# A graph network with two feed-forwards on one core: the last phase with its row preparation placed among the feed-forward's chunks, and the choice of rows by a search for the threshold

## What is computed

```
# _L1_gnn_ref, the end (out: 3125 x 4 heads x 64, divided by the sum of the edge weights)
out = jax.nn.elu(out + b)
x = x + out.reshape(N, 256)

# _L1_ffn_ref on the layer-normed x (b = 1, s = 3125)
weights = x @ wr + br
k = max(1, int(0.5 * s));  kk = k - 1                 # 1561 rows are kept
idx = top_k(weights, k)[:kk]                          # ties: the earlier row first
h = gelu(x[idx] @ w1 + b1);  y = (h @ w2 + b2) * weights[idx]
out = x_normed + (y put at idx, 0 elsewhere)          # and the layer's input is added to it
```

## Time and profile before

| | |
|---|---|
| median of 3 runs | 2442.72 us (2441.84 to 2443.51) |
| the profiled execution | 2447.71 us, its span 2446.0 us |
| busy in the span | PE 1842.6, DVE 1503.4, POOL 1372.5, ACT 627.9 us |
| last phase | from about 2152 us to the end |

### The profile page before, as it was taken

One profiled execution on the slowest core, in us unless ns is written; L12 is line 12 of the kernel. 1 busy time (PEld: TensorE's weight loads), 2 busy tenths in 40 slices (PEclk: granted clock), 3 DMA queues, 4 the chain that ended last, 5 costly groups with the idle time before them and its releaser, 6 DMA issues. The chain is left out here.

```text
span 2446.0 us, 37019 instructions
## 1 busy us (share of the span) xinstructions
PE 1842.6 (75%) x9564; PEld 1312.8 (54%) x9565; DVE 1503.4 (61%) x3325; ACT 627.9 (26%) x1252; POOL 1372.5 (56%) x1387
## 2 busy tenths in 40 slices
PE   2879999988997977109999995368888888811687
PEld 2667777763443447106666663256566566601366
DVE  7666644447557867713333333647777777678698
ACT  4000000004546654513333332121111111111342
POOL 3777777762777740464445445847777777632000
PEclk8565555558998987559999998569988989855798
DMA  7333333333002024321111111321111111300100
GB/s 226 105 101 103 105 104 104 105 97 116 1 1 54 1 75 158 97 75 35 37 35 39 37 37 44 89 64 28 28 28 28 28 28 28 27 5 0 26 26 28
DMA packets 113005, 144.03 MB, mean 59 GB/s; under 512 B 46718, under 2 KB 82430, under 8 KB 112822
## 3 DMA queue, kind: packets, MB, share of 16 engines
q0 software_dynamic: 60160, 86.81, 14.8%
q1 hardware_dynamic: 52787, 56.58, 7.7%
HBM read 114.00 MB, written 29.18 MB: 59 GB/s over the span
## 5 line engine op out<-in xcount | busy, mean ns | idle before, releaser
L497 PE MATMUL psA<-oh,G 128*128 128x128 f32 x1568 | 444.9, 448 | 64.0 <-DMA G<-xn_d,gat_i 34.3
L595 POOL DMA_INDIRECT rec_d<-rec,posd x392 | 393.4, 1004 | 167.2 <-issue 124.6
L1500 POOL DMA_INDIRECT g<-tab_d,recs x416 | 395.8, 951 | 148.6 <-issue 126.5
L312 POOL DMA_INDIRECT G<-xn_d,gat_i x392 | 379.5, 968 | 146.4 <-issue 138.8
L497 PEld LDWEIGHTS psA<-oh,G 128*128 128x128 f32 x1568 | 351.2, 312 | 157.5 <-issue 98.3
L1649 PE MATMUL psS<-vv,oh 128*125 128x260 f32 x832 | 290.1, 496 | 92.7 <-DVE acc L1581 92.5
L840 PE MATMUL psZ<-z,W 128*128 (+1 forms) x1344 | 264.1, 359 | 26.0 <-DVE z L739 26.0
L447 DVE TENSOR_TENSOR accT<-accT,psA 128x256 f32 x392 | 165.0, 421 | 170.4 <-PE psA L497 144.3
L1649 PEld LDWEIGHTS psS<-vv,oh 128*125 128x125 f32 x832 | 162.1, 226 | 190.7 <-DVE acc L1581 163.0
L642 ACT ACTIVATE z<-psZ,vec 128x500 f32 (+2 forms) x112 | 70.8, 634 | 643.1 <-PE psZ L833 533.3
L1246 PE MATMUL psH<-we,xh 128*128 x1344 | 215.1, 310 | 0.7 <-issue 0.6
(11 more groups left out here) (257 smaller groups left out, 2760.1 us busy)
## 6 DMA issues: line engine op xcount, KB each, us to landing
raw<-in_L_ffn_w SPq DMA_DIRECT2D x16, 682.0 KB, 10.2
xs_d<-zero SPq DMA_DIRECT2D x1, 7168.0 KB, 23.8
xs<-xs_d SPq DMA_DIRECT2D x56, 128.0 KB, 2.1
y_d<-yv POOLq DMA_DIRECT2D x56, 128.0 KB, 2.0
g<-tab_d,recs POOLq DMA_INDIRECT x416, 2.5
G<-xn_d,gat_i POOLq DMA_INDIRECT x392, 2.7
rec_d<-rec,posd POOLq DMA_INDIRECT x392
raw<-in_L_ffn_w SPq DMA_DIRECT2D x16, 384.0 KB, 10.1
```

The lines of the kernel that those rows point to most:

```text
L312: pool.indirect_dma_start(out=G[:, i, :], out_offset=None, in_=xn_d, in_offset=bass.IndirectOffsetOnAxis(ap=gat_i[:, t:t + 1], axis=0)).th ...
L497: last = nc.tensor.matmul(psA[i // 2][:, i % 2, h, :], G[:, i, 128 * h:128 * (h + 1)], oh[:, i, :], start=True, stop=True)
L595: pool.indirect_dma_start(out=rec_d.rearrange("p (t r) -> (p t) r", r=2), out_offset=bass.IndirectOffsetOnAxis(ap=posd[:, t:t + 1], axis=0 ...
L1500: pool.indirect_dma_start(out=g3[:, n % BODY, j, :], out_offset=None, in_=tab_d, in_offset=bass.IndirectOffsetOnAxis(ap=recs[:, t, 1:2], a ...
```

## The change

Phase 6 is written anew; the numbers of its operations per block stay as they are, but the order and some engines change.

- The five small loads are issued by SP at the start of phase 5.
- VectorE divides and adds `bgb` + 1 (it now does the add as well) for all five groups first (`lift`), ACT takes exp(og - 1) (`lifted`, four buffers `eg`). Then `fold(c)` finishes the ELU in two operations and makes mean and variance of group c; `spread`, `scales6` and `norm` give the square root (ACT), reciprocal, its value plus 1 and the offset (VectorE), and the normed rows (ACT, no longer VectorE). `twice(c)`, on ACT, makes x2 + xn4 as x2 (1 + 1/sd) - mean/sd in place of POOL's add.
- Only group 0 is prepared ahead of the feed-forward. Group c + 1 is prepared during chunk c (c < 4), its parts placed behind fixed m in each queue. Blocks are turned in pairs.
- The ranks and the trip through memory are gone. From chunk 4 on a search finds the value of the KEPT-th logit: one round counts the logits of one sign, eight rounds find the bits of the value, 3 and then 4 at a time; in each VectorE counts over its 25 logits a row for 7 or 15 candidates, and TensorE sums over the rows by a matmul with ones (`total`). A last round counts the values above and settles ties. Count, total and the reading of it are placed one m apart.
- `finish` is split: `lower` frees `psD` at once, and `finish` of blocks 0 to 15 follows in chunk 5, of 16 to 24 at the end.
- The downs of chunk 0 stand in front of chunk 1's ups; from chunk 2 on they stand among the ups as before. The writes of the output go in two parts, partitions 0 to 111 and 112 to 124.

The core of the diff (tile addresses, semaphores and the single operations of the search are left out):

```diff
@@ phase 5
+            @block.sync
+            def _(sp):
+                sp.dma_start(bgb[:, :], a["L1_gnn_b"].partition_broadcast(PB)).then_inc(s_b6, 16)
...
@@ phase 6, sync
-                sp.wait_ge(s_wv, 1)
-                    sp.dma_start(w_d.rearrange("o (b p) -> p (o b)", p=PB), wv[:, :]).then_inc(s_wd, 16)
-                sp.wait_ge(s_wd, 16)
-                sp.dma_start(wb[:, :], w_d[0, :].partition_broadcast(PB)).then_inc(s_wbl, 16)
                 for b0, n in CHUNKS:
                     sp.wait_ge(s_fin, b0 + n)
-                    sp.dma_start(ov[:, b0:b0 + n, :], outb[:, b0:b0 + n, :]).then_inc(s_out, 16)
+                    for lo, hi in SPLIT:
+                        sp.dma_start(ov[lo:hi, b0:b0 + n, :], outb[lo:hi, b0:b0 + n, :]).then_inc(s_out, 16)
@@ gpsimd: both loops of adds are gone; it fills less1, earlier, ones6 and tab
@@ scalar
+                def lifted(c):
+                    act.wait_ge(s_og, c + 1)
+                    if c >= 4:
+                        act.wait_ge(s_fold, c - 3)
+                    nc.scalar.activation(eg[:, c % 4, :, :], og[:, 5 * c:5 * c + 5, :], ACT.Exp, bias=less1[:, :]).then_inc(s_eg, 1)
+                def spread(c):
+                    act.wait_ge(s_v6, c + 1)
+                    nc.scalar.activation(sd6[:, 5 * c:5 * c + 5], mv6[:, 5 * c:5 * c + 5, 1], ACT.Sqrt).then_inc(s_d6, 1)
+                def norm(c):
+                    act.wait_ge(s_sc6, c + 1)
+                    for b in range(5 * c, 5 * c + 5):
+                        nc.scalar.activation(xn4[:, b, :], x2[:, b, :], ACT.Identity, bias=nm6[:, b:b + 1],
+                                             scale=rs6[:, b:b + 1]).then_inc(s_n6, 1)
+                for c in range(5):
+                    lifted(c)
+                spread(0)
+                norm(0)
+                for g in range(3):
+                    high_x(g)
                 for c, (b0, nb) in enumerate(CHUNKS):
                     for m in range(FM):
...
+                        if c < 4:
+                            if m == 1:
+                                spread(c + 1)
+                            if m == 2:
+                                norm(c + 1)
+                            if m == 4:
+                                high_x(3 * c + 3)
+                                high_x(3 * c + 4)
+                            if m == 6:
+                                high_x(3 * c + 5)
+                        if c < 5 and m == 7:
+                            twice(c)
@@ vector
+                def lift(c):
+                    ch.step(nc.vector.tensor_tensor(o_, v[:, hs, 0:OD], den[:, hs].unsqueeze(2).to_broadcast([PB, 5 * NH, OD]),
+                                                    ALU.mult))
+                    nc.vector.tensor_tensor(o_, o_, bgb[:, :].unsqueeze(1).to_broadcast([PB, 5 * NH, OD]), ALU.add).then_inc(s_og, 1)
+                def fold(c):
+                    ch.step(nc.vector.scalar_tensor_tensor(e_, e_, 1.0, og[:, cs, :], ALU.min, ALU.max))
+                    ch.step(nc.vector.scalar_tensor_tensor(x2[:, cs, :], e_, -1.0, x2[:, cs, :], ALU.add, ALU.add))
+                    dve.sem_inc(s_fold, 1)
+                    for b in range(5):
+                        ch.mark(nc.vector.bn_stats(bst6[:, b, :], x2[:, 5 * c + b, :]))
...
+                def digit_count(k):
+                    ch.step(nc.vector.tensor_tensor(met[:, 0:n, :], mag[:, :].unsqueeze(1).to_broadcast([PB, n, NB]),
+                                                    now.unsqueeze(2).to_broadcast([PB, n, NB]), ALU.is_ge))
+                    nc.vector.tensor_reduce(cn[:, 0:n], met[:, 0:n, :], AX_X, ALU.add).then_inc(s_cn, 1)
+                def digit_known(k):
+                    dve.wait_ge(s_cs, k + 2)
+                    ch.step(nc.vector.tensor_scalar(met[:, 0, 0:n], psC[:, 0:n], few[:, 2:3], 0.0, ALU.is_ge, ALU.add,
+                                                    accum_out=few[:, 3:4]))
...
                     for m in range(FM):
+                        fine(c, m, n)
                         n += 1
+                        if c < 4:
+                            if m == 0:
+                                fold(c + 1)
+                            if m == 1:
+                                scales6(c + 1)
+                            if m == 3:
+                                logits(c + 1)
+                            if m == 4:
+                                low_x(3 * c + 3)
+                                low_x(3 * c + 4)
+                            if m == 6:
+                                low_x(3 * c + 5)
+                        if c >= 2 and m % 2 == 1:
+                            lower(b0 - CB + m // 2)
+                        k = (c - SEARCH) * FM + m
+                        if k == 0:
+                            sign_count()
+                        if k == 1:
+                            sign_known()
+                            digit_count(0)
+                        if 2 <= k <= len(DIGITS):
+                            digit_known(k - 2)
+                            digit_count(k - 1)
+                        if k == ROUNDS:
+                            digit_known(ROUNDS - 2)
+                            last_count()
+                        if k == ROUNDS + 1:
+                            chosen()
+                        if k > ROUNDS + 1 and k - ROUNDS - 2 < b0 // CB - 1:
+                            for b in range(CB * (k - ROUNDS - 2), CB * (k - ROUNDS - 1)):
+                                finish(b)
@@ tensor
+                def total(r):
+                    n = 1 if r == 0 else DIGITS[r - 1][1] if r < ROUNDS else 1 + NB
+                    pe.wait_ge(s_cn, r + 1)
+                    last = nc.tensor.matmul(psC[:, 0:n], ones6[:, :], cn[:, 0:n], start=True, stop=True)
...
                 for c, (b0, nb) in enumerate(CHUNKS):
+                    if c == 1:
+                        for b in range(CB):
+                            down(b)
                     for m in range(FM):
+                        up(c, m, n)
                         n += 1
-                        if c and m % 2 == 1:
+                        if c >= 2 and m % 2 == 1:
                             down(b0 - CB + m // 2)
+                        if c < 4 and m == 3:
+                            turn6(3 * c + 3)
+                            turn6(3 * c + 4)
+                        if c < 4 and m == 5:
+                            turn6(3 * c + 5)
+                        r = (c - SEARCH) * FM + m - 1
+                        if 0 <= r <= ROUNDS:
+                            total(r)
```

More of the change, by code:

```diff
@@ new lines, in program @@
+        ones6 = at("ones6", o, [PB, PB]); o += 512
+        DIGITS = [(28, 7)] + [(sh, 15) for sh in range(24, -1, -4)]
+        tab = at("tab", o, [PB, len(DIGITS), 16], I32); o += 512
+        cand = at("cand", o, [PB, 16], I32); o += 64
+        met = at("met", o, [PB, 16, NB]); o += 1600
+        cn = at("cn", o, [PB, 1 + NB]); o += 128
+        few = at("few", o, [PB, 8]); o += 32
+        dig_i = at("dig_i", o, [PB, 1], I32); o += 32
+        pre_i = at("pre_i", o, [PB, 1], I32); o += 32
@@ L1755, in _ @@
+                nc.gpsimd.memset(less1[:, :], -1.0).then_inc(s_k6, 1)
+                ch.n += 1
                 ch.step(nc.gpsimd.memset(earlier[:, :], 1.0))
[L1756 to L1767, removed]
+                ch.step(nc.gpsimd.affine_select(out=earlier[:, :], in_=earlier[:, :], compare_op=ALU.is_gt, fill=0.0,
+                                                base=0, pattern=[[1, PB]], channel_multiplier=-1))
+                ch.step(nc.gpsimd.memset(ones6[:, :], 1.0))
@@ L1769, in _ @@
+                for k, (sh, n) in enumerate(DIGITS):
+                    ch.step(nc.gpsimd.tensor_scalar(tab[:, k, 0:n], iota[0:PB, 1:1 + n], float(1 << sh), None, ALU.mult))
             @block.scalar
             def _(act):
-                for c in range(5):
[L1772 to L1781, removed]
@@ new lines, in norm, with twice @@
+                def norm(c):
[3 more added lines that the diff above has]
+                                             scale=rs6[:, b:b + 1]).then_inc(s_n6, 1)
+                def twice(c):
+                    for b in range(5 * c, 5 * c + 5):
+                        nc.scalar.activation(x2[:, b, :], x2[:, b, :], ACT.Identity, bias=nm6[:, b:b + 1],
+                                             scale=rp6[:, b:b + 1]).then_inc(s_x6, 1)
@@ L1783, in _, with high_x @@
+                def high_x(g):
+                    act.wait_ge(s_t6, g + 1)
+                    t, cols = turned(g)
+                    nc.scalar.activation(xt6[:, 0, :, cols], t, ACT.Copy, scale=XS).then_inc(s_th, 1)
+                act.wait_ge(s_k6, 1)
+                for c in range(5):
+                    lifted(c)
[3 more added lines that the diff above has]
+                    high_x(g)
                 n = 0
-                act.wait_ge(s_b6, 80)
@@ new lines, in finish @@
```

(18 more changed lines are left out.)

253 lines of the change are left out of this document (150 added, 103 removed).

## The result

The changed kernel takes 2362.3 us (median of 4 runs, 2360.0 to 2364.0), 0.9667 of the kernel before (95% interval 0.965 to 0.9684). The forecast was 2366. A second measurement gave 0.9658 (0.9645 to 0.9671). The profiled execution took 2362.4, its span 2360.7.

A forecast was written before the change was run, and what follows sets the result against it. VectorE was taken to set the feed-forward's pace, after 115 us before the first gelu. Steps from 2152.4 plus 3 for the clock reached 2369.5, 76.5 under 2446.0; off the 2442.7 median, 2366 us; 8-in-10 range 2350 to 2396.

The forecast's parts named there:

- head, to the first up: Start of the last phase: no wait for loads, only group 0 prepared; 27.4 us, first up-projection at 2179.8.
- chunk 0: First feed-forward chunk: three engines take turns, 21.8 us, then four downs alone; 38.3 us in all, to 2218.1.
- chunk 1: Second chunk: same chain without downs and first load, 21.8 us plus 1.3 for its first up, to 2241.2.
- chunks 2 and 3: Downs among ups, rest of row preparation partly showing: 27 us each, 54 together; bounds 22.0 and 30.0 each.
- chunk 4: First chunk with the search: four pairs of positions at about 6.3 us, 25.2 us.
- chunk 5: Second search chunk: one 6.3 us pair, three of 5.15, 1.2 for chosen; 22.9 us, sixteen finishes under TensorE.
- chunk 6 to the last finish: Last chunk: ups, downs and down(24) 15.8 us, then drain and finishes; 17.8 us, last finish at 2361.1.
- last finish to the end: Output writes after the last finish: old 5.4 us kept, 2 either way put in the range.
- allowance for the clock: 3 us added to the summed path for clock dips, moving the end from 2366.5 to 2369.5.
- Table loads: Square root and gelu alternate on ACT in chunks 0 to 3: eight more loads, 10.3 us, about 7 showing.
- The search: Nine rounds in chunks 4 and 5: odd positions hidden by the down; a pair takes about 6.3 instead of 5.15 us.
- rival (a): TensorE's clock holds only in part: a chunk takes 44 instead of 27 us; one gives 2383, two 2400; chance 0.20.

## Why the prediction was right, and which terms were off

The forecast for the length of the phase was 217.1 us (from 2152.4 to 2369.5). By its own steps, in us:

| step | forecast | measured |
|---|---|---|
| head, to the first up | 27.4 | 27.9 |
| chunk 0 | 38.3 | 37.0 |
| chunk 1 | 23.1 | 22.7 |
| chunks 2 and 3 | 54.0 | 54.1 (29.0 and 25.1) |
| chunk 4 | 25.2 | 24.9 |
| chunk 5 | 22.9 | 23.1 |
| chunk 6 to the last finish | 17.8 | 17.8 |
| last finish to the end | 5.4 | 3.9 |
| allowance for the clock | 3.0 | no row of its own: about 1.4, inside chunk 2 |
| phase | 217.1 | 211.4 |

The last finish here ends at 2356.8:

```profile
2356.31 0.48 DVE L1976 SCALAR_TENSOR_TENSOR outb<-xn,wk,x 125x256 f32<-125x256 f32 x1
```

**The head** held as worked out. VectorE's ten operations took 1.49 us each. POOL's filling of its small table, which I had not priced, took 1.27 us an operation, 10.1 in all, and cost VectorE nothing.

**The chain of chunks 0 and 1** was right in its links: fold holds ACT's square root, the load back to gelu and the norm hold the gelus behind them, and the downs stand alone. Moving fold and moving the downs shortened the phase by 3.1 and 9.4.

**Table loads.** Ten, as forecast. I let about 7 us of them show, and 5.6 did: the load before each square root ran while ACT waited for fold.

**Chunks 2 and 3.** The sum held, the parts didn't, and that is luck: chunk 2 was 2.0 over my 27 and chunk 3 was 1.9 under it. TensorE stood 4.6 us for normed rows in chunk 2 and 2.0 in chunk 3. My sentence that no wait in chunks 2 to 6 was longer than 4 us was too bold by 0.6.

**The search.** A pair took 6.7, not 6.3: I left out TensorE's totals themselves, which cost 0.13 and 0.24 us of its time. But only three pairs took that long, the ones before and behind them 6.1 and 6.2, and the chunks came out right. The cause, the total in the even position, was shown by moving it. VectorE was busy 81% of chunk 5, a little more than the 80% that I gave as its bound, with the sixteen finishes under TensorE.

**The end.** I left the old 5.4 us for two late writes of 500 KB. It took 3.9. While the last writes ran, the DMA engines were busy 0.33 and moved 107 GB/s before (2440.0 to 2444.5), and 0.92 and 256 GB/s here (2356.0 to 2359.0). So the writes in two parts went more than twice as fast, which leaves room for the second write of 500 KB. That the split at 112 partitions did it is the likely reading, but it was not tried by itself.

**The clock.** The granted clock was 0.85, 0.77 and 0.88 in chunks 0, 1 and 2, and 1.00 in chunks 3 to 5. So rival (a) shows in the clock, and very little in the time. In chunks 0 and 1 ACT and VectorE set the pace. In chunk 2 a part is on TensorE's path, behind the wait of 4.6 us; the same work in chunk 3 stands below it:

```profile
2253.95 4.14 PE L2053 MATMUL psU<-xt,f 128*128 128x500 f16 x12
2257.93 2.78 PE L2065 MATMUL psD<-f,fh 128*125 128x256 f16 x24
...
2280.10 2.70 PE L2053 MATMUL psU<-xt,f 128*128 128x500 f16 x12
2282.63 2.78 PE L2065 MATMUL psD<-f,fh 128*125 128x256 f16 x24
```

From up to down are 3.98 us there and 2.53 here, 1.4 more. It is inside the 29.0 of chunk 2, so the separate 3.0 us weren't needed. With 1.5 at the end and 1.7 in chunks 0 and 1, less 0.5 at the head, they are the 5.7 us by which the phase was shorter than forecast. One reading in the prediction was loose: where it says that at 90% busy the clock was up, the row has TensorE at 78.8 of 92 us, 86%, at a clock of 0.94.

**Where the 82 us came from** is what the forecast's path did not say. The experiments give: the loads 6.3; the choice of rows 45.1 from the kernel before, of which the search gives back 7.1, so 38.0; placing the rows among the chunks 8.5. What is left is 29.4. With all rows prepared in front the first up comes 74.6 us into the phase. In the kernel before it comes at 110.5, and with only the loads moved at 104.1, which is 29.5 more than 74.6. So that remainder is the leaner preparation (norm and the last addition on ACT, the bias on VectorE without POOL beside it, ELU in two operations, blocks turned in pairs). Which of these made how much was not tried. The loads and the choice were measured in the old order and the search and the placing in the new one; that the remainder agrees with the two heads within 0.1 us speaks for adding them up, though no run shows it for each by itself.

## What to carry to other kernels

Work moved off the head of a phase and in among its loop is only hidden as far as the loop's bound is another engine *at each link*: here 47 us of preparation went in and 38 came out again as longer chunks, because each part stood behind a fixed step of three queues. Start such work a step earlier than it is needed, spread matmuls that stand alone among others, and put a cross-engine round behind, not in front of, the independent work that can cover it; these moves of a few lines gave 27 us more. When a large rewrite lands on its forecast, take its parts away one by one all the same: here the part with the most code to place gave least but for the loads.

## What the runs showed of the hardware that I had not expected

POOL's first add or multiply after the short fills at the start of the phase began some 7.4 us behind them: 7.45 in the changed kernel, 7.32 with only the loads moved, 6.9 to 7.9 in the others that don't wait for the loads there. The profile shows no wait on another engine in it; at its start stand two records MODIFY_POOL_CONFIG of POOL's queue (2150.2 in the changed kernel). In the kernel with only the loads moved this held the head up, by the 4.07 us shown above. The 9.8 us in the earlier trace rows is another case: there POOL had to wait for the loads and for VectorE's first product as well.

POOL's multiply of 125 x 15 values with an integer result took 1.27 us on average, where a reduction of 12 values a row takes VectorE 0.17. Beside it VectorE's two-input operations kept their 1.49 us, while beside POOL's adds over 1280 elements the same took 4.16.
